# Later scatter numbers, three quarters of a weight cast on VectorE, and a weight subtraction behind the scatter

## The reference

```python
scores = softmax(x @ gate_w.T)                      # 16 experts
topk_w, topk_ids = lax.top_k(scores, 6)
topk_w = topk_w / (topk_w.sum(-1, keepdims=True) + 1e-20)
combine = einsum('tk,tke->te', topk_w, one_hot(topk_ids, 16))
def body(acc, ew):                                  # for each expert
    w13_e, w2_e, c_e = ew
    g, u = split(x @ w13_e.T, 2)                    # 512 -> 2 x 352
    return acc + c_e[:, None] * ((silu(g) * u) @ w2_e.T)   # 352 -> 512
out = out + swiglu(x, sw13, sw2)                    # shared, on all tokens
x = x + tanh(g_ffn) * out
```

## Time and profile before

| | |
|---|---|
| Median of three runs | 1419.17 us |
| Profiled execution | 1422.3 us, span 1420.5 us |
| TensorE busy in the span | 1307.5 us (92%) |
| VectorE / ScalarE / GpSimd busy | 60% / 51% / 67% |
| Granted TensorE clock, mean | 0.971 |
| Routed tiles | from about 714 us to the end |

### The profile page before, as it was taken

The page is one execution under the profiler, slowest core; times in us unless marked ns, Lnnn a source line. Parts: engine busy times, 40 slices in busy tenths (PEclk is TensorE's granted clock), DMA queues, the critical chain, the costliest instruction groups (busy, mean ns, idle before and its releaser), DMA issues.

```text
span 1420.5 us, 31069 instructions
## 1 busy us (share of the span) xinstructions
PE 1307.5 (92%) x8064; PEld 1175.1 (83%) x8065; DVE 851.5 (60%) x1570; ACT 729.5 (51%) x1317; POOL 944.7 (67%) x671
## 2 busy tenths in 40 slices
PE   7897998998988899999789999999999999999995
PEld 2676887887888789999678988888988898888895
DVE  5879888897989865653244444444444445444441
ACT  5898887988879554343233333333333333333331
POOL 0589898999888847888366556666556665556722
PEclk8899999998999999999999999999999999999999
DMA  4121122223242555655487878887878778877752
GB/s 138 34 73 38 54 68 97 68 68 97 69 130 61 145 142 105 141 100 129 92 246 209 213 185 214 219 213 210 216 181 220 214 199 221 210 191 212 203 134 37
DMA packets 136276, 205.91 MB, mean 145 GB/s; under 512 B 20496, under 2 KB 74384, under 8 KB 134016
## 3 DMA queue, kind: packets, MB, share of 16 engines
q1 hardware_dynamic: 101744, 102.33, 23.8%
q0 software_dynamic: 31024, 62.10, 23.6%
q10 hardware_dynamic: 3440, 40.63, 8.1%
HBM read 130.99 MB, written 76.25 MB: 146 GB/s over the span
## 4 chain that ended last, share of the span: by engine, by line
PE 33%; POOL 12%; issue 9%; DMA 8%; DVE 4%; ACT 2%; POOLq 1%; ACTq 1%; DVEq 0%
PE bank L1814 11%; PE bank L1794 9%; PE bank L1795 9%; DMA out_x<-ys,aid 7%; POOL token_lists L1086 6%; POOL w L1046 4%; PE bank L1805 2%; POOL out_x L1068 1%; DVE hs L1236 1%; ACT w L876 1%; PE bank L1704 1%; PE bank L1690 1%; DVE xl L1439 1%; DMA out_x<-ys 1%; POOLq L1091 1%
## 5 line engine op out<-in xcount | busy, mean ns | idle before, releaser
L1794 PE MATMUL bank<-w,xh 128*128 (+1 forms) x1088 | 365.3, 337 | 26.0 <-DVE xl L1439 24.5
L1008 POOL TENSOR_TENSOR hc<-hs,crow 128x512 f32<-128x512 f32 x254 | 322.1, 1302 | 91.8 <-DVE hs L1236 86.2
L1795 PE MATMUL bank<-w,xh 128*128 (+1 forms) x1088 | 351.3, 323 | 0.0
L1074 POOL DMA_INDIRECT out_x<-ys,aid x104 | 165.2, 1589 | 254.6 <-issue 226.4
L1236 DVE TENSOR_TENSOR_SCAN hs<-dA,bank 128x512 f32<-128x512 f32 x256 | 295.7, 1208 | 50.3 <-PE bank L1704 31.6
L1814 PE MATMUL bank<-w,ah 128*128 (+1 forms) x816 | 259.3, 399 | 15.3 <-DVE al L1485 15.3
L1485 DVE TENSOR_TENSOR al<-bank,ah 128x384 fp32r<-128x384 f32 x136 | 75.8, 558 | 294.9 <-ACT ah L921 279.7
L1794 PEld LDWEIGHTS bank<-w,xh 128*128 128x128 f32 x1088 | 204.7, 188 | 42.5 <-issue 34.3
L927 ACT COPY ys<-bank 128x512 f32<-128x512 f32 x136 | 79.9, 587 | 262.8 <-PE bank L1814 262.8
L1795 PEld LDWEIGHTS bank<-w,xh 128*128 128x128 f32 x1088 | 206.7, 190 | 4.5
L1814 PEld LDWEIGHTS bank<-w,ah 128*128 128x128 f32 x816 | 150.2, 189 | 44.0 <-issue 12.9
(11 more groups left out here) (184 smaller groups left out, 1983.6 us busy)
## 6 DMA issues: line engine op xcount, KB each, us to landing
raws<-in_wall ACTq DMA_DIRECT2D x16, 2176.0 KB, 8.9
token_quarters<-xt SPq DMA_DIRECT2D x104, 256.0 KB
xs<-token_quarters SPq DMA_DIRECT2D x104, 256.0 KB, 3.2
crow<-c_rows SPq DMA_DIRECT2D x64, 256.0 KB, 3.3
xt<-token_rows_turned SPq DMA_DIRECT2D x32, 256.0 KB, 2.9
out_x<-ys POOLq DMA_DIRECT2D x32, 256.0 KB, 4.2
token_rows<-rowb SPq DMA_DIRECT2D x4, 1028.0 KB, 5.9
xrow<-in_x SPq DMA_DIRECT2D x4, 1024.0 KB, 8.0
```

The lines of the kernel that those rows point to most:

```text
L1008: nc.gpsimd.tensor_tensor(hc[:, j, :], hs[:, j, :], crow[:, n % 4, :], ALU.mult).then_inc(hc_done, 1)
L1074: pool.indirect_dma_start(out_rows, bass.IndirectOffsetOnAxis(ap=aid[:, s:s + 1], axis=0), ys[:, s, :], None, bounds_check=TOKENS - 1, oob ...
L1794: nc.tensor.matmul(gate_bank[:, 0:I], xx, columns(w, off + ww + k * 2 * I, I), start=first, stop=last)
L1795: mm = nc.tensor.matmul(up_bank[:, 0:I], xx, columns(w, off + ww + k * 2 * I + I, I), start=first, stop=last)
```

## The change

`SHARE` is three quarters: VectorE casts 3264 columns of a coming set and ScalarE 1088. On GpSimd `next_weights`, with its subtraction, moves from ahead of `expert_starts` and `add` to behind them, in the loop and in the eight tiles after it. On VectorE the copy to `aid` for tile t+1, which stood between `keep_ids` and the writing of `gid`, goes, and a copy for tile t stands behind `multiply(t)`.

```diff
--- before.py
+++ after.py
@@ -60,7 +60,7 @@
 NT = TILES + 8
 NR = E * TT + 16
 HALF = TT // 2
-SHARE = WCOLS // 2
+SHARE = 3 * WCOLS // 4
 PEELED = NS - 1
 AHEAD = 7
 TAKEN = AHEAD - 4
@@ -1127,17 +1127,17 @@
                     t = 4 * i + NS + k
                     gather(t + AHEAD, (k + AHEAD) % 4, i + (k + AHEAD - 4) // 4)
                     number = starting_set(t)
-                    next_weights(number)
                     expert_starts(number, t, k)
                     add(t, k)
+                    next_weights(number)
             rest = tiles_but_12(pool) + 4
             for k in range(8):
                 if k + AHEAD < 8:
                     gather(rest + k + AHEAD, (k + AHEAD) % 4, looped + (k + AHEAD - 4) // 4)
                 number = starting_set(rest + k)
-                next_weights(number)
                 expert_starts(number, rest + k, k % 4)
                 add(rest + k, k % 4)
+                next_weights(number)
 
 
         @block.vector
@@ -1551,8 +1551,6 @@
                 if takes and not plain:
                     take_weight(t + TAKEN, slot_of(TAKEN), number, group_of(TAKEN))
                     keep_ids(t + TAKEN, slot_of(TAKEN))
-                if not static or t + 1 >= NS:
-                    add_ids(t + 1, slot_of(1))
                 if static and t < NS:
                     for late in FIRST_ROWS.get(t, ()):
                         if late >= NS + 4:
@@ -1563,6 +1561,8 @@
                     gather_ids(t + AHEAD, slot_of(AHEAD), column)
                 x_low(t + 1, 1 - s)
                 multiply(t, place % 4)
+                if not static or t >= NS:
+                    add_ids(t, place % 4)
                 if not static or t >= PEELED:
                     next_weights(t, split)
 
@@ -1602,6 +1602,7 @@
                 tile(last - 4 + k, 3 + k, looped, k < 2, False)
             a_low(last - 1, 0)
             multiply(last, 3)
+            add_ids(last, 3)
             a_low(last, 1)
 
 
```

## The result

| | before | after |
|---|---|---|
| Median | 1419.14 us (6 runs, 1417.9 to 1422.58) | 1406.51 us (6 runs, 1402.07 to 1412.19) |
| Ratio, 95% interval | | 0.9913 [0.9885, 0.9942] |
| Profiled execution | 1422.3 us, span 1420.5 us | 1408.32 us, span 1406.6 us |
| Granted TensorE clock, mean | 0.971 | 0.973 |

The change made the kernel faster, by 12.6 us (0.9%) and not by the 33 forecast; 1406.5 lies outside the range of 1382 to 1400.

What follows compares the result with a forecast made beforehand. The prediction took TensorE as the bound, at 6.283 us a routed tile, plus 35.6 us of stalls. Removing these, less 2.3 us left or new, gains 33.3 us: median 1419.17 to 1386 us, range 1382 to 1400.

Steps and rivals of the forecast that it cites:

- the 35.6 us: TensorE's stalls over 101 routed tiles, 2.37 us an expert, from waits for `al` and for scatters ahead of `xl`.
- the new lateness: GpSimd's subtraction behind the scatter delays the next gather, store and load; shown expert's stall at VectorE's turn 0.6 us.
- `cc` of t+8: VectorE's copy needing the gather queued behind the subtraction, eight tiles past the expert's first; stall 0 to 0.6 us.
- the term of 0.1 us an expert: Average stall from GpSimd's late queue: 0.6 us in one expert of six.
- At 9.3, halfway, all of this is 0.7 us earlier and the last stall is just gone: With the previous tile's scatter landing in 9.3 us, VectorE's turn no longer stalls, against 0.6 in the shown expert.
- caught up five tiles later, before the next expert: GpSimd's queue behind the subtraction, at 3.2 us a pair, is served before the next expert, six or seven tiles on.
- a growth of landings: Failure sign: landing of the gather, the load or the previous tile's scatter growing by over 1 us.
- The cast: ScalarE's part shrinks to 1.106 us, VectorE's grows to 1.94; the 0.75 us stall on `al` goes, 0.05 stays.
- The lock-out: VectorE's longer cast holds up GpSimd's DMA issue; unpriced, bounds 0 to 0.6 us; as rival 1392 us, chance 0.08.
- Backlog stalls: Rival: subtraction, gather, store, load exceed their spare in most experts; 1 us an expert gives 1399 us; chance 0.18.
- Only the cast counts: Rival: the scatter's wait reappears on VectorE, so only 11 us are gained, 1408 us; chance 0.04.
- Slower: the gather lands late: Rival: gather behind the subtraction lands late, stalling `cc` and VectorE's turn 4.6 us an expert; 1454 us, chance 0.05.

Runs made afterwards that it cites:

- e1: Kernel after without GpSimd's part: subtraction ahead of the wait and scatter as before, three-quarter cast and late `aid` copy kept; 1389.07 us, ratio 0.9758.
- e2: Kernel before with only the late `aid` copy added; 1398.11 us, ratio 0.9830.
- e3: Kernel before with only GpSimd's new order, `next_weights` behind `add`; 1515.31 us, ratio 1.0659.
- e6: Kernel after with ScalarE's load of the next weights issued two tiles later; 1397.67 us, ratio 0.9816 against before.
- e7: e1 with the subtraction cut in two, first half ahead of the wait, second behind `add`; 1387.05 us, ratio 0.9751 against before.
- e4: Kernel before with only the cast's split changed, `SHARE` three quarters; 1430.28 us, ratio 1.0056.
- e5: Kernel after with `SHARE` back at one half, so late `aid` and GpSimd's new order only; 1410.28 us, ratio 0.9908 against before.

## Why the prediction was wrong

**Right: what the 35.6 us were.** e1 has 1.0 us left, so all of it could go, and by the two causes named: `al` (e2 leaves just that) and the waits for scatters ahead of `xl`.

**Right: the new lateness, its path and its deadline.** The forecast let the gather of t+8 go out at 998.6, 25.1 us after t+1, for a stall of 0.6, and at 24.4 for none. In the kernel after gathers up to 24.6 us stall nothing at t+6; the one at 25.1 costs 0.95 and the one at 25.5 costs 1.6. The consumer that costs most is the one named, VectorE's turn of t+7; the weights cost nothing. The forecast also named `cc` of t+8, with 0 to 0.6 us, and the tiles t+5 and t+6 as the place to look. `cc` has its share, 3.0 us in the tiles t+5.

**Wrong: the term of 0.1 us an expert for it.** It rests on the step "At 9.3, halfway, all of this is 0.7 us earlier and the last stall is just gone", on the one that let GpSimd have "caught up five tiles later, before the next expert", and so on the weights load making the same landing as before. Measured, the gather of t+8 goes out at 23.0 to 27.8 us, 25.75 on average. All stalls but those of t+1 are 21.3 us, 1.4 an expert instead of 0.1; without the one tile of 6.3 us, told below, 1.0.

The reason is in the spread. With seven tiles to the expert before (seven of these experts), the scatter of t goes out at 11.7 to 14.1 us, 13.1 on average, about as forecast (12.9 at the halfway landing, 13.6 in the shown expert). With six (seven experts) it goes out at 15.1 to 16.4, 15.6 on average. After six tiles the backlog of the last subtraction is not yet served: GpSimd's rows above show pairs back to back at 922 to 929, where the earlier trace rows have an idle 3.75 us before the scatter at 975.90. There the scatter of t-1 goes out 2.9 us after t+1 instead of 2.4. But that is one expert: in the six others after six tiles it goes out at 2.0 to 2.4, and what is longer is its landing. Beside the weights load and the late stores and loads of the backlog it takes 11.1 to 13.0 us after six tiles, 12.0 on average, and 8.5 to 10.9 after seven. Before, it took 9.5 to 10.1 and 8.5 to 9.7. In these six SP issues four stores and loads between 0.2 and 8.4 us after t+1, and two before the change.

The lateness feeds itself from expert to expert; I worked out one expert from an undisturbed start. Two runs speak for it. e3 has the same order on GpSimd, but its experts stall so long (7.5 to 10.0 us each, after the first one) that the queue has drained by the next: there the landing after six tiles is 9.5 to 9.9 us, as before. e6, which takes the load away, breaks the loop. What part of the longer landing the stores and what part the scatters make was not measured.

**A single large loss.** 6.3 us of the 26.6 are one tile, t+2 of the expert at 1219.25, which runs from 1225.62 to 1238.23. VectorE's turn there, kernel after:

```profile
1233.22 0.73 DVE L1432 STREAM_TRANSPOSE bank<-xs 128x512 f32<-128x512 f32 x1 [8.15 <-DMA xs<-token_quarters]
```

Its load was issued at 1219.75, 1.7 us before the weights load, and landed 13.3 us later. In before the longest such landing was 10.4 us. No other kernel here has such a tile, and whether the change causes it or one execution had it is open. The forecast listed a growth of landings as what would make it fail, and gave it no price.

**The cast: right in size, with a rest that was not seen.** VectorE's took 1.86 us (1.94 forecast) and ScalarE's 1.10 (1.106). In e1 no stall stays. In the kernel after t+1 is late in six experts by 0.46 to 0.98 us, 4.6 us in all with the smaller ones, against 0.75 forecast (0.05 each). There ScalarE's read of the table was slow. Its timeline, and the chain of 962 to 971 us:

```profile
964.20 0.58 ACT L927 COPY ys<-bank 128x512 f32<-128x512 f32 x1 [2.22 <-PE bank L1815]
966.35 1.10 ACT L876 CAST w<-raws  x1 [1.57 <-issue]
```

```profile
964.29 1.25 ACTq L931
```

The cast starts 2.15 us behind the start of `ys`, where it was 1.20 before (`ys` at 973.95, the cast at 975.15), since the read took 1.25 us instead of a median of 0.28. This holds throughout: at this place the read took 0.77 to 1.25 us in the seven experts that lose 0.23 to 0.99 us in t+1, and 0.28 to 0.32 in the seven that lose nothing. So the 4.6 us are the read's, and with a read of usual length the new split left nothing. Why the read is slow is not settled; e1 and e7, where no tile waits for `xs`, show next to none of it (one stall of 0.42 in e7, with a read of 0.96).

**The lock-out: there, and not the main cost.** I gave it no price and 0 to 0.6 us as bounds. The scatter of t-1, issued inside VectorE's cast, takes 1.87 to 1.93 us instead of 1.59 wherever it starts 2.0 us behind t+1, and the gather at 924.06 took 2.45 instead of 0.99, ending 0.12 us behind the cast (926.51 against 926.39). So an issue inside the cast is held until its end. The row at 721.47, which I set against this, could not show it: that scatter ended 0.5 us behind a cast of 1.29 us anyway. In the kernel after the same one, at 716.85 inside the cast of 716.05 to 717.91, took 1.18 us instead of 0.99 and ended at 718.03, again 0.12 behind. The Trainium skill ("SBUF — State Buffer", section "SBUF: two separate sides") has a GpSimd DMA blocked until VectorE's end and about 115 ns more; the 0.12 us agree. In e1 this happens at nearly each expert and no tile is late. In e4, where the scatter of t is still waited for, it has a small price: the subtraction starts 5.25 us after t+1 instead of 4.95 and the scatter of t goes out at 15.0 instead of 14.7, and it adds some of the up to 0.35 us that most experts lose there. In a queue that is late already, as at 924.06, it adds up to 1.5 us, and that part of the loss I could not take apart from the backlog.

**The rivals.** Backlog stalls, given 0.18, is what happened; priced there at 1 us an expert and 1399, it was 1.0, and 1.4 with the one large loss; its range of 1390 to 1400 was missed all the same, by that loss and the 4.6 us in t+1. "Only the cast counts" forecast 1408, near the time by chance, and is refuted by e2: the waits for scatters did go. "Slower: the gather lands late" had the places right, but the gathers behind the subtraction whose landing can be told took 3.2 to 3.4 us, and what came late was their issue.

## What to carry to other kernels

A wait and a long instruction on one engine that overlap cost the longer of the two, and in the other order the sum: before moving work behind a wait, add up what stands behind both, and compare with the start that the work had. When a step's spare is under the spread of a landing, take the distribution over all experts, and the short ones first, since a queue that has not drained makes the next landing later. Take the parts of such a change apart: here two of three make 0.9758, and the third gave some 1.5% back.

The kernel to keep is e1 or e7, at 1389.07 and 1387.05 us; their intervals overlap. Both beat the kernel before and the kernel after.

## What the runs showed of the hardware

- A scatter of 128 rows lands in 4.0 to 6.7 us (e6) where the load of 2.2 MB is not beside it, in 8.4 to 10.8 where it is (e1, e7), and in 11.0 to 13.0 with a backlog as well (after and e5, behind six tiles). The weights load itself took 8.3, 8.9 and 11.9 us (min, median, max) before, and 8.2, 10.7 and 11.8 after.
- ScalarE's read of one table number took 0.28 us in the median and up to 1.25 in the kernel after, up to 1.40 in e6.
- A DMA that GpSimd issues inside a VectorE cast of 1.86 us ends its record 0.12 us behind the cast (gather 2.45 us instead of 0.99, plain scatter 1.18 instead of 0.99) where it would have ended sooner.
- GpSimd's subtraction of 4352 columns takes 9.6 us alone; its record is 10.18 us long where it starts 1.0 us after a scatter's, and overlaps it.
